# Moving the second attention's mask, the low halves and the routing choice between engines in a fused attention and expert kernel

## What is computed

```python
x = x + xattn(layernorm(x), ctx, ctx, Wq, bq, Wk, bk, Wv, bv, Wo, bo)   # 16 heads, 77 context rows, causal
h = layernorm(x)      # the second attention runs over the 8 sequences, for each position by itself
ln1 = layer_norm(h); qkv = ln1 @ qkv_weight.T   # 16 query heads, 4 key/value groups
scores = where(causal, q @ k.T / sqrt(32), min) # the second mask
h1 = h + (softmax(scores) @ v) @ proj_weight.T
y = layer_norm(h1); probs = softmax(y @ router_weight)
# the two best experts of each token, at most 1280 tokens for an expert in order of arrival
moe[e] = gelu(y[tokens of e] @ w1[e]) @ w2[e]
out = x + h1 + sum of moe * share
```

## Time and profile before

| | us |
|---|---|
| median of 3 runs (lowest, highest) | 1609.86 (1607.93, 1612.03) |
| the profiled execution | 1610.14 |
| its span | 1608.3 |
| PE busy, share of the span | 1503.3, 93% |
| DVE, ACT, POOL busy | 918.7, 711.1, 836.4 |
| granted clock, mean over the span | 0.968 of full |

### The profile page before, as it was taken

One profiled execution on the slowest core, in us unless ns is written; L12 is line 12 of the kernel. 1 busy time (PEld: TensorE's weight loads), 2 busy tenths in 40 slices (PEclk: granted clock), 3 DMA queues, 4 the chain that ended last, 5 costly groups with the idle time before them and its releaser, 6 DMA issues. The chain is left out here.

```text
span 1608.3 us, 31118 instructions
## 1 busy us (share of the span) xinstructions
PE 1503.3 (93%) x11079; PEld 1319.9 (82%) x11080; DVE 918.7 (57%) x1736; ACT 711.1 (44%) x1425; POOL 836.4 (52%) x953
## 2 busy tenths in 40 slices
PE   8888889999999999998958998999999899999986
PEld 6677778888888888777748897999999789999876
DVE  3657656777887766788765445432333653443361
ACT  2445544555555555465414344432333543342341
POOL 2444544666665555687635466633432766454232
PEclk9899999999999999999968999999999999999998
DMA  7212211222222212122223234433433533433221
GB/s 259 62 57 80 80 53 41 73 75 72 78 71 71 67 56 72 67 92 80 76 75 112 59 87 101 108 78 81 94 61 55 132 81 102 87 93 53 31 35 24
DMA packets 64400, 125.94 MB, mean 78 GB/s; under 512 B 13369, under 2 KB 13785, under 8 KB 63724
## 3 DMA queue, kind: packets, MB, share of 16 engines
q1 hardware_dynamic: 45932, 93.80, 17.8%
q0 software_dynamic: 17920, 29.31, 10.5%
q10 hardware_dynamic: 384, 0.61, 0.1%
HBM read 89.12 MB, written 46.27 MB: 84 GB/s over the span
## 5 line engine op out<-in xcount | busy, mean ns | idle before, releaser
L1445 PEld LDWEIGHTS hidden_ps<-gT,w 128*128 128x128 f32 x2880 | 350.0, 192 | 9.4 <-ACT hT L1362 4.2
L1445 PE MATMUL hidden_ps<-gT,w 128*128 128x256 f32 x2880 | 352.2, 284 | 5.8 <-ACT hT L1362 3.4
L1475 PE MATMUL expert_ps<-w,hT 128*128 128x512 f32 x1440 | 342.8, 398 | 8.1 <-DVE og L1412 8.1
L1475 PEld LDWEIGHTS expert_ps<-w,hT 128*128 128x128 f32 x1440 | 273.1, 191 | 66.5 <-DVE og L1412 8.9
L1244 POOL TENSOR_TENSOR w<-raw,w 128x1024 fp32r<-128x1024 f32 x64 | 157.8, 2512 | 262.1 <-ACT w L1238 262.1
L1387 DVE TENSOR_TENSOR hT<-gl,hT 128x512 fp32r<-128x512 f32 x160 | 126.7, 800 | 251.6 <-ACT hT L1362 251.6
L1360 ACT ACTIVATE gl<-hidden_ps 128x512 f32<-128x512 f32 x160 | 95.7, 598 | 331.6 <-PE hidden_ps L1445 308.1
L1341 POOL DMA_INDIRECT out_dram<-og,idx x80 | 129.3, 1617 | 75.0 <-DVE og L1412 45.6
L1412 DVE TENSOR_SCALAR og<-expert_ps,kept 128x512 f32<-128x512 f32 x80 | 59.3, 749 | 159.4 <-PE expert_ps L1475 150.9
L1370 ACT ACTIVATE gT<-yk 128x256 fp32r<-128x256 f32 x160 | 66.9, 418 | 124.9 <-DVE yk L1398 123.5
L1332 POOL DMA_INDIRECT xg<-normed_tokens,idx x80 | 89.0, 1113 | 58.8 <-POOL idx L1327 30.5
(11 more groups left out here) (179 smaller groups left out, 3091.3 us busy)
## 6 DMA issues: line engine op xcount, KB each, us to landing
raw<-L_ffn_moe_w_dram SPq DMA_DIRECT2D x64, 512.0 KB, 3.5
normed_tokens<-h SPq DMA_DIRECT2D x128, 65.0 KB
xa<-x_dram SPq DMA_DIRECT2D x32, 256.0 KB, 2.7
xc<-x_dram SPq DMA_DIRECT2D x32, 256.0 KB, 3.0
attended_rows<-x SPq DMA_DIRECT2D x32, 256.0 KB, 2.1
fx<-attended_rows SPq DMA_DIRECT2D x128, 64.0 KB
out_dram<-fx SPq DMA_DIRECT2D x128, 64.0 KB
fx<-qkv_rows_dram SPq DMA_DIRECT2D x1, 1536.0 KB, 6.6
```

The source lines that it names most:

```text
L1445: last = pe.matmul(pH[:, q, f * W:(f + 1) * W], w1[p][l][:, k, cols], xT[g.s % 2][r][:, k, :], start=k == 0 and n == 0, stop=k == KT - 1 a ...
L1475: last = pe.matmul(pY[:, k, :], hT[par][l][:, f, k * P:(k + 1) * P], w2[p][r][:, f, :], start=f == 0 and n == 0, stop=f == FT - 1 and n == 2)
```

## The change

It moves work; what is computed stays.

- *Second mask.* Up to step LATE the mask matmul is left out; DVE adds a 32-wide mask from SBUF to the scores in PSUM ahead of the row maximum. The matmul stays in the steps after LATE.
- *Low halves.* `low_halves` is split into `low_attended` (for `wo`) and `low_normed` (for `xt`, wanted by `q`). Up to step FF the one that PE wants first in the next step is made ahead of the first difference L943 of the scores (for the first eight tiles) or between its two halves; the other one follows at the end of the step. In step 15 both stand right behind the transpositions of the keys, ahead of the statistics and sums.
- *Step 15 and banks.* In step 15 `zt` comes after `wo` on PE, `xt` and `pt` keep their own banks, and ACT writes the high half of `pv` ahead of the exponentials in step 14.
- *Choice.* The three batches of 9 tiles in steps 42, 44 and 46 become one batch of 26 tiles, in three parts in steps 45, 46 and 47; a batch of 5 follows in step 50. The counts move to match.
- *First expert's pieces.* Pieces 4 to 7 come one step earlier, and DVE instead of POOL makes the low halves of pieces 6 and 7, at the start of steps 49 and 50.
- *POOL.* After LATE the residual sum (L512) is made ahead of the wait for the statistics.
- *Logits.* The lg matmuls wait for each quarter of `y2` on its own.
- *Experts.* The first group's gathers read the row table itself and the copy follows; group 1 is turned after the first quarter of group 0's first products instead of before them.
- Four one-column work buffers become one.

The diff, cut to its core:

```diff
-EARLY_LOW = FF
+EARLY_LOW = FF + 1
-FIRST_PIECES = {LATE: (0,), LATE + 2: (1,), LATE + 4: (2,), LATE + 6: (3,), LATE + 8: (4,), LATE + 9: (5,),
-                LATE + 10: (6,), LATE + 11: (7,)}
+FIRST_PIECES = {LATE: (0,), LATE + 2: (1,), LATE + 4: (2,), LATE + 6: (3,), LATE + 7: (4,), LATE + 8: (5,),
+                LATE + 9: (6,), LATE + 10: (7,)}
+LATE_LOW = {LATE + 11: 6, LATE + 12: 7}
-CHOICES = ((STEPS - 10, 0, 9), (STEPS - 8, 9, 18), (STEPS - 6, 18, 27), (STEPS - 2, 27, 31), (STEPS, 31, 32))
-COUNTS = {STEPS - 5: (0, 6, 1), STEPS - 4: (6, 13, 2), STEPS - 3: (13, 21, 3), STEPS - 2: (21, 27, 3),
-          STEPS - 1: (27, 31, 4)}
+CHOICES = {STEPS - 7: (0, 26, 0), STEPS - 6: (0, 26, 1), STEPS - 5: (0, 26, 2), STEPS - 2: (26, 31, None)}
+COUNTS = {STEPS - 4: (0, 9, 1), STEPS - 3: (9, 18, 1), STEPS - 2: (18, 26, 1), STEPS - 1: (26, 31, 2)}
...
-    jobs += [("zt", fz, 0, 0), ("wo", tw, 0, 1), ("s2", fs, 0, 1), ("o2", fo, 0, 1)]
+    jobs += [("wo", tw, 0, 1), ("zt", fz, 0, 0)] if i == FF + 1 else [("zt", fz, 0, 0), ("wo", tw, 0, 1)]
+    jobs += [("s2", fs, 0, 1), ("o2", fo, 0, 1)]
...
-            if i <= FF and kind != "s":
+            if kind != "s" and (i <= FF or (i == FF + 1 and kind in ("xt", "pt"))):
...
# POOL
+                    if i > LATE:
+                        residual(f)
                     pool.wait_ge(s["stat_h"], f + 1)
...
                 for j in FIRST_PIECES.get(i - 1, ()):
-                    weights["low"](pool, 0, 0, j)
+                    if j < 6:
+                        weights["low"](pool, 0, 0, j)
# ACT
-                if i < FF:
+                if i <= FF:
                     high_halves(i)
...
# DVE
+                if i in LATE_LOW:
+                    dve.wait_ge(weights["counts"]["w_lo"], LATE_LOW[i])
+                    weights["low"](dve, 0, 0, LATE_LOW[i])
...
                     need(dve, s["p2t_mm"], f)
+                    if i <= LATE:
+                        chained(dve.tensor_tensor(scores, scores, bc(tmask, 1, [P, 16, TB]), ALU.add))
                     chained(dve.tensor_reduce(nm2[:, :], scores, X, ALU.max, negate=True))
...
                     for half in range(2):
+                        if i <= FF and half == (0 if t < S else 1):
+                            sooner(i + 1)
                         dve.tensor_tensor(pr[:, t % 2, 2 * half:2 * half + 2, :, :],
...
                     k_turn.then_inc(s["k_turned"], 1)
+                if i == EARLY_LOW:
+                    low_normed(i + 1)
+                    low_attended(i + 1)
...
-                if i < EARLY_LOW:
-                    low_halves(i + 1)
+                if i <= FF:
+                    if t is None:
+                        sooner(i + 1)
+                    later(i + 1)
# PE
-                    pe.matmul(bank("s2", fs), token_sel[:, :], token_mask[:, :], start=True, stop=False)
+                    if i > LATE:
+                        pe.matmul(bank("s2", fs), token_sel[:, :], token_mask[:, :], start=True, stop=False)
...
                     if fr is not None:
+                        pe.wait_ge(s["y2_done"], 4 * fr + k + 1)
...
# experts
+                            if isinstance(c, int) and c == 0 and i == 6 and q == 0:
+                                turn_rows(c, 5)
...
+                if not (isinstance(c, int) and c == 0 and i == 5):
+                    turn_rows(c, i)
```

More of the change, by code:

```diff
@@ L207, in psum_plan @@
 def psum_plan():
-    place, ousted, user, turn = {}, {}, [None] * 8, [0, 0]
+    place, ousted, user, turn = {}, {}, [None] * 8, [0, 3]
     def take(job, banks):
@@ L234, in build_main @@
 def build_main(nc, a, x2d, mid, out2d, z2d, small, logits, tops, choice, row_table, weights, groups, sb, sem):
-    ident, ln1w, ln1b, ln2w, ln2b, bq, bk, mask, blocks = (
-        small[n] for n in ("ident", "ln1w", "ln1b", "ln2w", "ln2b", "bq", "bk", "mask", "blocks"))
+    ident, ln1w, ln1b, ln2w, ln2b, bq, bk, mask, blocks, tmask = (
+        small[n] for n in ("ident", "ln1w", "ln1b", "ln2w", "ln2b", "bq", "bk", "mask", "blocks", "tmask"))
     wr = small["wr"].rearrange("p (k e) -> p k e", e=E)
@@ L293, in build_main @@
     mvx, mvf, mvh = sb("mvx", [P, 2, 2]), sb("mvf", [P, 2, 2]), sb("mvh", [P, 2, 2])
-    wx, wf, wh = sb("wx", [P, 1]), sb("wf", [P, 2]), sb("wh", [P, 1])
+    ones = sb("work", [P, 4])
+    wx, wh, share_sum, expo2 = (ones[:, n:n + 1] for n in range(4))
+    wf = sb("wf", [P, 2])
     rx, shift_x, rf, rh = sb("rx", [P, 2]), sb("shift_x", [P, 2]), sb("rf", [P, 8, 2]), sb("rh", [P, 2])
@@ L1421, in _, with turn_rows @@
         def _(pe):
+            def turn_rows(c, i):
+                g = At(c, i - 4, PER)
+                if g.within(NG):
+                    need(pe, s["yk_done"], g.count(KT))
+                    for k in range(GB):
+                        pe.wait_ge(gathered[g.s % 2][k], g.turns(2, 16, 16))
+                        for m in range(KT):
+                            last = pe.transpose(pT[:, k, m * P:(m + 1) * P], xg[:, g.s % 2, k, m * P:(m + 1) * P],
+                                                ident[:, :])
+                    last.then_inc(s["xt_mm"], 1)
             def first_row(g):
@@ L1452, in step @@
                         pe.sem_inc(s["fc1_mm"], 4)
-                g = At(c, i - 4, PER)
-                if g.within(NG):
-                    need(pe, s["yk_done"], g.count(KT))
-                    for k in range(GB):
-                        pe.wait_ge(gathered[g.s % 2][k], g.turns(2, 16, 16))
-                        for m in range(KT):
-                            last = pe.transpose(pT[:, k, m * P:(m + 1) * P], xg[:, g.s % 2, k, m * P:(m + 1) * P],
-                                                ident[:, :])
-                    last.then_inc(s["xt_mm"], 1)
+                if not (isinstance(c, int) and c == 0 and i == 5):
+                    turn_rows(c, i)
                 g = At(c, i - 7, PER)
@@ L1528 @@
     pieces["wr"] = rows(np.asarray(inputs["L0_ffn_router_weight"])).reshape(P, KT * E)
-    pieces.update({name: tables.pop(name) for name in ("ident", "mask", "blocks")})
+    pieces.update({name: tables.pop(name) for name in ("ident", "mask", "blocks", "tmask")})
     laid["small"] = np.concatenate([pieces[name] for name, _ in SMALL_WIDTHS], axis=1)
```

111 lines of the change are left out of this document (67 added, 44 removed).

## The result

The changed kernel took 1588.99 us in the median of 4 runs (1583.60 to 1590.34); the kernel before took 1609.41 us beside it. The ratio is 0.9865, with a 95% interval from 0.9839 to 0.9891: 20.4 us faster by the medians, where 19.6 us were forecast. The profiled execution is the 1583.60 us one and has a span of 1581.8 us; a second profiled execution of the same kernel took 1586.37 us (span 1584.6). Of all 8 runs the median is 1588.5 us.

What follows compares the result with a forecast made beforehand. PE waits for DVE in the cross tiles, PE and an equally long DVE chain bind the middle, DVE and POOL the last steps, PE the experts; terms sum to -19.6 us from 1610.1, so 1590.5, median 1590.3, range 1576 to 1601.

Steps and rivals of the forecast that it cites:

- Low halves, steps 2 to 13: Cross tiles: making the half PE wants earlier removes its waits for DVE, -7.1 us (bounds -4 and -8).
- what ends last then is PE's own turning of the shares, so the 5.8 us go in full: Cross tiles, before the query products: PE's six waits for the low half of turned x vanish entirely, 5.8 us.
- The second rival: Cross tiles: the chain through exponentials, sums and shares is as long as the one cut; 1599 us, chance 0.15.
- The clock: Query blocks up to step 16: two of three clock falls behind PE's waits vanish, -3.0 us (bounds 0 and -6).
- The rival for which I cited it: Middle steps: the mask gives PE a gap in each of 23 steps and the clock falls there; 1625 us, chance 0.05.
- Steps 14 to 16: Step 16's low halves ahead of statistics, sums and z remove a 3.8 us wait; step 15 counted 0; -3.8 us.
- Second mask: 23 steps: PE saves 0.52 us, DVE's equally long chain grows 0.73; +3.3 us in all (bounds -12.0 and +4.8).
- Choice: Steps 42 and 44: moving the batches away saves 2.5 us in each, -5.0 us (bounds -2 and -6.5).
- Last logits: End of the steps: unblocked difference, POOL's earlier residual and logits by quarters, -0.8 us (bounds +1.5 and -3).
- Experts' start: First gather 1.1 us sooner, group 0's products no longer behind group 1's turning; -3.2 us (bounds -1 and -4.5).
- everything after is PE's row, so it stays: Experts, after the first products: PE is the bound, so the 3.2 us gained at the start are kept.
- PE alone as the bound: Middle steps: pv's 0.15 us is chance, so the mask gives its full -12.0 us; 1575 us, chance 0.13.

Runs made afterwards that it cites:

- the two-by-two table: Changed kernel, a step of the middle with second mask on PE or DVE: queries turned behind the sums 21.89 or 21.96 us, ahead of them 21.88 or 21.27 us.

## Why the prediction was right, and where it was not

The total came out within 1 us of the forecast because errors of both signs met, and that they met so closely is luck. By its steps:

- **Low halves, steps 2 to 13 (-7.1 forecast with a separate term for the clock; -5.3 and a clock share of 3.1 measured).** The term was sized 1.8 us too large. The step that failed is "what ends last then is PE's own turning of the shares, so the 5.8 us go in full". In step 9 of the change the low half is ready at 128.40 + 0.69 = 129.09 us, and PE starts the query products at 130.65:

```profile
128.40 0.69 DVE L873 TENSOR_TENSOR xT_lo<-main_ps,xT_hi 128x512 fp32r<-128x512 f32 x1
129.01 1.50 DVE L971 TENSOR_TENSOR pr<-main_ps,nm 128x616 f32<-128x616 f32 x2
130.65 0.36 PE L364 MATMUL main_ps<-xT_hi,wq_hi 128*128 128x256 f32 x1 [1.25 <-DVE pr L971]
```

  The queries go into banks 0 and 1, which the cross scores hold until the differences have read them (130.51 us). I looked at when the operand was ready and not at when the destination was free. From the mask to the query products it was 136.16 - 130.45 = 5.71 us, and is 130.65 - 125.45 = 5.20: 0.5 us gained of the 1.36 that I booked (the mask L958 starts at 125.45). Taking for each step a profile without a fall (the kernel before, the one with the low halves back, or the one with the experts' start alone), the distances from step 4 to 13 shrank by 4.0 us in sum; the other 3.1 are the clock. The sixth wait lies between steps 13 and 14, and there the change gives 1.3 us (15.33 us before, 14.03 after, 15.29 with the low halves back). So 1.8 of the 7.1 us did not come, and the new wait for the differences, four times, 4.9 us in all, is what stands in their place. The second rival came true to that part, through the differences and not through the exponentials.
- **The clock (-3.0 forecast).** Between 60 and 260 us the kernel before has five falls to half, and so have the two kernels that share its first stage. The change has two in both profiles, and the same code with pieces 6 and 7 on POOL only one. A step with a fall is 1.6 us longer than the same step without (14.31 and 12.69 us for step 14 to 15). Three falls less are 4.8 us, inside my bounds of 0 and 6; I had counted two. That falls went is no luck: all four profiles with the late low halves have two between 60 and 180 us, and the nine with the early ones have none or one. How many are left in step 15 to 17 varies from kernel to kernel. The rule of the Trainium skill ("TensorE: Matmul & The Clock Gate", Part 1, the throttled state is the default and activity releases it) agrees with the start of the experts above. The rival for which I cited it, a fall at each gap of the middle, did not come: 15 gaps of 0.6 us at a granted clock of 1.00.
- **Steps 14 to 16 (-3.8 forecast).** The wait went as I said, but two others came. The cross scores of step 15 wait 1.7 us, by the times shown for the bank of `zt`, a candidate that I had seen and bounded at +1; and the wait for ACT's copy of the turned shares, 3.0 us in place of one of 2.2 us for DVE, I had not seen. Undone alone, the edits of step 15 are worth 1.7 to 1.8 us.
- **Second mask (+3.3 forecast; -1.0 and -1.2 measured, the change's two profiles against the mask back on PE, from the cross scores of step 15 to the scores of s2 in step 38).** The mechanism is shown by the two-by-two table, and `pv` stood 0.15 us behind the turned queries in all 15 steps as forecast; the size was off in two terms. PE saves 0.62 us and not 0.52 a step: 2.73 - 2.11 us, as shown above, since the eight score matmuls, which now open their bank instead of adding to it, took 496.12 - 495.24 = 0.88 in place of 496.53 - 495.53 = 1.00 us. DVE's chain behind the addition is 0.06 us shorter (503.82 - 497.06 = 6.76 against 517.20 - 510.38 = 6.82 us). 0.74 - 0.62 - 0.06 = 0.06 us a step, and 0.07 was measured, in place of 0.21. And I carried the price over all 23 steps: in step 16 (0.6 us) and in steps 34 to 38 (1.5 us) PE keeps its gain.
- **Choice (-5.0 forecast, -6.3 and -7.3).** I booked 2.5 us for each of two steps; they gave 2.7 and 3.2. The rest is a step of 13.4 us ahead of them (41 to 42), which is 12.4 and 11.7 us in two other kernels with the same code up to there, and 11.65 and 12.45 us in the two profiles of the change: chance. The cause was mixed: I named the blocked product, which was a third of the price. The other two thirds stayed with an unblocked batch in steps 43 and 45, and no run shows what makes a batch dear there and cheap in step 46.
- **Last logits (-0.8 forecast, +0.4 and +0.5).** The blocked operation went, but DVE stood 3.58 us for ACT's half, and its piece and the batch of five come behind that. So the last difference ends 31.65 us behind the scores of step 47, where the blocked one ended after 31.24 us: my count that the new train ends when the blocked difference ended was right to 0.4 us. Of what I booked on top of it one part came, in the next row of the table. The blocked operation of the slots is short again (before, after):

```profile
824.76 0.92 DVE L791 TENSOR_SCALAR over<-within 128x64 f32<-128x64 f32 x1
```

```profile
802.76 0.20 DVE L808 TENSOR_SCALAR over<-within 128x64 f32<-128x64 f32 x1
```

  The slots are 0.7 us shorter by it in both profiles, so -0.3 and -0.2 us stand against the -0.8. The gain from POOL's earlier residual and the logits by quarters does not show. And DVE's piece blocks POOL in turn: the small operation L569 takes 1.40 us beside it, and 0.41 us elsewhere. That is the rule of the Trainium skill ("SBUF — State Buffer", "Who interferes with whom") that I had weighed; it came true on two operations of POOL, about 1 us each.
- **Experts' start (-3.2 forecast, 0.2 to 2.1 as measured alone).** Two steps of it failed. The first is the 1.1 us for the gather. From the last operation of the table to the first gather it was 842.69 - 840.83 = 1.86 us and is 819.68 - 818.11 = 1.57:

```profile
840.83 0.20 DVE L828 CAST rows<-token 128x80 int32<-128x80 f32 x1
```

```profile
818.11 0.20 DVE L845 CAST rows<-token 128x80 int32<-128x80 f32 x1
819.68 1.32 POOL L1375 DMA_INDIRECT xg<-normed_tokens,rows  x1 [18.35 <-issue]
```

  So the copy cost 0.3 us; I had taken the 0.94 us between copy and gather for a price of the copy, and the gather needs most of it without one too. From the same operation of the table the first products come 2.8 and 3.2 us sooner than before, in place of 4.2. The second step is "everything after is PE's row, so it stays". Behind the 1.0 us for the turning, which I had booked, the products ran 0.6 to 0.8 us longer at half clock in the two profiles of the change, and 3.6 us longer in the kernel with the new start alone; half of that is lost, 0.3 to 1.8 us. At the second products -1.4 and -1.9 us are left.

Of the rivals, PE alone as the bound is ruled out for the order of DVE in this change, and is true once the queries are turned first. In the cross tiles no run shows a loss beyond the 1.8 us above.

## What to carry to other kernels

When two engines' chains are equally long, moving work from one to the other is worth nothing, whichever looks busier; shorten the chain of the receiving engine first, by putting what frees a bank ahead of what nobody waits for, and the same move brings its full price. Before booking a wait as gone, look for the second condition of the waiting instruction, above all whether its destination bank is free. An earlier start out of a quiet stretch pays less than it moves, as long as the clock is still down. And a gap between two operations is the price of the first only if the second starts sooner without it.

## What the runs showed of the hardware

- One addition of 128x512 from PSUM and a broadcast SBUF operand costs DVE 0.74 us from start to start. A mask matmul of 32 rows costs PE 0.62 us in all, of which 0.1 us is in the eight matmuls that then add to its bank (496.53 - 495.53 against 496.12 - 495.24 us).
- After the quiet stretch of the slots, the clock came back 1.9 to 2.9 us behind the start of the dense products with the later start, and 3.2 to 6.5 us with the earlier one.
- DVE and POOL block each other in both directions: single 0.16 us operations of DVE took 1.43 and 2.08 us beside POOL's 128x1024 subtraction, and a 0.41 us one of POOL took 1.40 us beside DVE's. The subtraction itself is 1.25 us on DVE and 2.35 us on POOL.
- The first gather of rows starts 1.57 us behind the start of the operation that makes its row numbers, and 1.86 us with a copy of 0.19 us between the two.
- The same program differs by up to 9 us from one execution to the next (1582.20 to 1591.16 us), while a step of the middle, where the clock is whole, repeats to 0.02 us (21.96 and 21.94 in the two profiles of the change).
